# Room for GpSimd's DMA descriptors: 2048 in place of 16384 bytes of a partition

## The chip, the core and the metric

The kernel runs on one core of one Trainium2 chip. The metric is device microseconds of one execution. Before the change the median of three timed runs is 4273.25 us (4268.43 to 4274.99).

The engines are called PE (TensorE; PEld is its loading of weights), DVE (VectorE), ACT (ScalarE), POOL (GpSimd) and SP (SyncE). Each runs its own list of instructions in order, and they wait for one another by semaphores. SP, ACT and POOL also issue DMAs; all of those run on the core's 16 DMA engines.

## What is computed

Two layers on graphs: 8 graphs of 2048 nodes with 256 features, and an adjacency matrix of 0 and 1 per graph.

```python
h = maximum(layernorm(x), 0)
idx = first 25 neighbours of each node, by number
agg = max over them of h[idx]               # maximum(agg, 0) where a node has 25 or fewer
x = x + relu(concat(h, agg) @ W0 + b0)

h = maximum(layernorm(x), 0)
hidden = h @ W1.T
s = leaky_relu(hidden @ a1 [row] + hidden @ a2 [column])
x = x + softmax(s over neighbours) @ hidden + bias
```

## The kernel before

The 16384 nodes are handled in 32 quads of 512 rows, four tiles of 128 rows each (one row per partition). A step s of the main loop takes quad s through layer 0 and quad s - 4 through the attention of layer 1, so that from step 4 on both go on beside one another (`LAG`, `STEPS`, lines 34 and 59). Steps 0 to 3 have no attention; the attention of the last five quads is done in a part of its own behind the loop, where step 31's gathers are the last.

Layer 0 needs, for each node, the normalised features of its 25 neighbours. They lie in a table in HBM, and POOL fetches them (lines 470 to 525): for each of the four tiles of a quad it issues 25 indirect DMAs, called gathers here, one for each place k in the list of neighbours. A gather reads 128 rows of 1 KB, one into each partition, at the addresses in `idx[:, t, k]`. That makes 100 gathers in a step and 3200 in all. Tiles alternate between two buffers `near[:, 0]` and `near[:, 1]` and two semaphores `near_in[0]` and `near_in[1]`, and every gather adds 16 to its tile's semaphore when it has landed. The core of it:

```python
for k in range(S):
    attention(s, stages, t, k)
    pool.indirect_dma_start(
        out=near[:, t % 2, k, :], out_offset=None, in_=table,
        in_offset=bass.IndirectOffsetOnAxis(ap=idx[:, t, k:k + 1], axis=0),
    ).then_inc(near_in[t % 2], 16)
```

Ahead of a tile POOL waits until DVE has read the tile before the last out of the same buffer (`agg_made`), and ahead of tiles 0 and 2 for their indices (`idx_ready`). `attention(s, stages, t, k)` (line 476) adds further waits ahead of fixed gathers: POOL isn't to run ahead of certain marks of the attention. In steps 5 to 30 they stand in tile 0 ahead of k = 3, 8, 12 and 20 and in tile 1 ahead of k = 4, 9 and 21; in steps 4 to 30 in tile 2 ahead of k = 16 and 22 and in tile 3 ahead of k = 1, 8, 16 and 22. None stands ahead of k = 13, the 14th gather, or k = 14, the 15th, of any tile.

DVE takes the maximum over a tile's 25 neighbours as soon as all have landed (`maximum`, line 910: `near_in[t % 2]` has to reach 16 x 25 more than for the tile before in that buffer; its first instruction is line 914). PE multiplies by the weights (line 1266), DVE adds the residual (line 933). Meanwhile DVE searches the next quad's neighbours (lines 851, 857), ACT makes the masks from the adjacency (line 566), and attention runs in eight chunks: SP transposes masks by DMA (line 364), ACT and PE make the weights (lines 596, 602, 1325, 1326), PE the products (line 1333).

[...]

## Time and profile before

| | us |
|---|---|
| timed runs, median of three | 4273.25 |
| timed runs, lowest and highest | 4268.43, 4274.99 |
| profiled execution, its span (the only time that its page gives) | 5229.9 |
| busy in the profiled execution: POOL | 3056.0 |
| busy: PE, DVE, ACT | 2607.8, 2599.4, 1568.6 |
| idle time of POOL ahead of gathers | 1944.2 |

The span goes from the first to the last instruction of the profiled execution. That execution is 957 us longer than the median of the timed runs, so a share or a wait that it shows can't be taken over into a timed run as it stands. A gather's busy time on POOL is the making of its descriptors, not the transfer; when a tile has landed is seen from DVE, which waits for it.

### The profile page before, as it was taken

The page shows a single profiled execution, that of the slowest core. Times are in us where ns is not written, and L with a number is a line of the kernel's source. Part 1 is how long each engine was busy: PE and PEld are TensorE (multiplying, and loading weights), DVE is VectorE, ACT ScalarE, POOL GpSimd, SP SyncE. Part 2 cuts the span into 40 slices and gives each one's busy share as a digit, 9 for nine tenths or more (in the row PEclk, how much of TensorE's full clock was granted, in tenths as well). Part 3 has the DMA queues.
Part 4 walks back from the last instruction along what each step waited for, and adds up shares of the span by engine and source line. Part 5 has one row for each costly group of instructions (what it writes and reads, how often), then busy time and mean ns, then how long its engine had stood idle before and what let it go on. Part 6 is the DMA issues. An engine that isn't in the chain of part 4 may idle for free.

```text
span 5229.9 us, 38170 instructions
## 1 busy us (share of the span) xinstructions
PE 2607.8 (50%) x8674; PEld 1604.8 (31%) x8782; DVE 2599.4 (50%) x6725; ACT 1568.6 (30%) x1745; POOL 3056.0 (58%) x3204
## 2 busy tenths in 40 slices
PE   2122235556455455545555545555554555553479
PEld 0011113333233333333333323333332333332256
DVE  5444354454455454555445546545455554544432
ACT  3011123323333323333323333332333333232135
POOL 5565556666666566666656666666666665666510
PEclk6555557777666777667777766777766777776689
DMA  7344446556655555565655655665566565555320
GB/s 253 114 162 141 144 139 188 160 181 181 176 180 177 168 178 170 178 189 170 187 155 178 184 178 168 188 178 172 170 178 188 170 187 157 171 175 154 121 88 29
DMA packets 477228, 866.03 MB, mean 166 GB/s; under 512 B 308298, under 2 KB 309204, under 8 KB 456660
## 3 DMA queue, kind: packets, MB, share of 16 engines
q0 software_dynamic: 153600, 419.64, 28.2%
q1 hardware_dynamic: 305140, 378.64, 22.5%
q10 hardware_dynamic: 18432, 67.12, 3.3%
q8 instruction: 22, 0.36, 0.0%
q14 instruction: 34, 0.28, 0.0%
HBM read 690.98 MB, written 119.54 MB: 155 GB/s over the span
## 4 chain that ended last, share of the span: by engine, by line
PE 26%; issue 23%; another core or an unknown queue 22%; DVE 17%; ACT 8%; SPq 2%; DMA 1%; POOL 1%; ACTq 0%; DVEq 0%; POOLq 0%
PE acc L1333 13%; DVE highest L917 6%; DVE lin L941 3%; PE bank L1266 3%; ACT nm_t L566 2%; ACT wgt L602 2%; PE pen L1326 2%; DVE top L851 2%; PE pen L1325 1%; PE bank L1246 1%; DVE key L857 1%; ACT pen L596 1%; PE bank L1283 1%; SPq L364 1%
## 5 line engine op out<-in xcount | busy, mean ns | idle before, releaser
L521 POOL DMA_INDIRECT near<-table_dram,idx x3200 | 3055.8, 955 | 1944.2 <-issue 1000.3
L1333 PE MATMUL acc<-hid,wgt 128*128 (+1 forms) x4096 | 1187.2, 442 | 458.8 <-ACT wgt L602 380.9
L1333 PEld LDWEIGHTS acc<-hid,wgt 128*128 128x128 f32 x4096 | 889.6, 223 | 643.7 <-issue 435.2
L917 DVE TENSOR_TENSOR highest<-near,highest 128x512 f32<-128x512 f32 x1280 | 889.8, 695 | 167.5 <-DVE highest L917 75.9
L933 DVE SCALAR_TENSOR_TENSOR x_q<-bank,x_q 128x256 f32<-128x256 f32 x128 | 54.2, 423 | 1269.6 <-PE bank L1268 1052.9
L602 ACT ACTIVATE wgt<-pen,a_slope 128x512 f32<-128x512 f32 x448 | 305.5, 682 | 984.6 <-remote 522.7
L1266 PE MATMUL bank<-w_sb,h_t 128*128 128x256 f32 x1024 | 381.0, 536 | 422.8 <-ACT h_t L692 314.1
L566 ACT ACTIVATE nm_t<-adj_i,big_c 128x2048 bf16<-128x2048 int32 x128 | 501.1, 3942 | 7.3 <-DMA adj_i<-in_adj_dram 4.8
L941 DVE CUSTOM_DVE_ANT_0 lin<-acc,nm_q 128x2048 bf16<-128x2048 f32 x108 | 247.5, 2291 | 385.6 <-ACT acc L713 382.8
L1275 PE MATMUL acc<-cst,wgt 128*128 128x128 f32 x248 | 61.0, 427 | 750.6 <-ACT wgt L577 680.8
L1266 PEld LDWEIGHTS bank<-w_sb,h_t 128*128 128x128 f32 x1024 | 261.1, 268 | 508.5 <-ACT h_t L692 333.4
L851 DVE MAX8 top<-key 128x8 f32<-128x256 f32 (+1 forms) x1024 | 356.0, 388 | 114.2 <-remote 84.6
L596 ACT ACTIVATE pen<-a_b,a_rise 128x512 f32<-128x512 f32 x448 | 307.6, 691 | 198.4 <-DMA nm_c<-nm_q 98.0
L692 ACT ACTIVATE h_t<-bank 128x512 f32<-128x512 f32 x128 | 75.9, 593 | 909.3 <-PE bank L1260 454.1
L577 ACT ACTIVATE wgt<-x_q,shift,rstd 128x256 f32<-128x256 f32 x124 | 64.3, 590 | 761.7 <-DVE shift L801 418.7
L1325 PE MATMUL pen<-m_r,ones_b 3*128 3x512 bf16 x432 | 196.7, 455 | 182.1 <-issue 125.7
L857 DVE MATCH_REPLACE8 key<-top,key 128x256 f32<-128x256 f32 (+1 forms) x768 | 287.0, 382 | 0.0
L1275 PEld LDWEIGHTS acc<-cst,wgt 128*128 128x128 f32 x248 | 48.6, 223 | 756.7 <-ACT wgt L577 686.2
L1258 PE MATMUL bank<-cst,h_q 128*128 128x128 f32 x256 | 66.2, 350 | 376.7 <-DVE key L872 157.2
L1246 PE MATMUL bank<-nm_t,bit_w 128*128 128x512 bf16 x512 | 180.5, 512 | 107.7 <-ACT nm_t L566 50.8
L914 DVE TENSOR_TENSOR highest<-near 128x512 f32<-128x512 f32 x128 | 89.9, 703 | 175.4 <-DMA near<-table_dram,idx 131.4
L1300 PE MATMUL bank<-lin,ones_f 128*128 128x512 f32 x54 | 55.9, 1139 | 237.8 <-DVE x_q L933 229.3
(148 smaller groups left out, 2253.8 us busy)
## 6 DMA issues: line engine op xcount, KB each, us to landing
adj_i<-in_adj_dram SPq DMA_DIRECT2D x128, 1024.0 KB
nmask_dram<-nm_t ACTq DMA_DIRECT2D x128, 512.0 KB
nm_q<-nmask_dram SPq DMA_DIRECT2D x29, 2048.0 KB
near<-table_dram,idx POOLq DMA_INDIRECT x3200
h_q<-table_dram SPq DMA_DIRECT2D x32, 512.0 KB
x_q<-in_x_dram SPq DMA_DIRECT2D x32, 512.0 KB
xmid_dram<-x_q SPq DMA_DIRECT2D x32, 512.0 KB
o_q<-xmid_dram SPq DMA_DIRECT2D x32, 512.0 KB
```

The source lines that it names most:

```text
L521: pool.indirect_dma_start(out=near[:, t % 2, k, :], out_offset=None, in_=table, in_offset=bass.IndirectOffsetOnAxis(ap=idx[:, t, k:k + 1], ...
L566: nc.scalar.activation(nm_t[:, u, :].rearrange("p (q t r) -> p q t r", q=QB, t=T), by_tile, ACT.Relu, bias=BIG_B, scale=-BIG).then_inc(nm_ ...
L596: nc.scalar.activation(pen[:, j % 2, :], row, ACT.Relu, bias=rises[:, j:j + 1], scale=RISE).then_inc(lin_made, 1)
L602: nc.scalar.activation(wgt_part(j), pen[:, j % 2, :], ACT.Exp, bias=slopes[:, j:j + 1]).then_inc(wgt_made, 1)
L851: nc.vector.max(top[:, u, 8 * r:8 * r + 8], src[:, u, :]).then_inc(ix_step, 1)
L857: nc.vector.match_replace(src[:, u, :], top[:, u, 8 * r:8 * r + 8], src[:, u, :], PADKEY).then_inc(ix_step, 1)
L917: nc.vector.tensor_tensor(highest[:, :], pair(k), highest[:, :], ALU.max).then_inc(mx_step, 1)
L941: nc.vector.tensor_tensor_reduce(out=scratch, in0=scores, in1=non_edges[:, t, :], scale=1.0, scalar=-3.0e38, op0=ALU.subtract, op1=ALU.max ...
L1246: mm = nc.tensor.matmul(words, bit_w[:, k, :], members[:, :, k % T, :, k // T], start=(k == 0), stop=(k == GB - 1))
L1266: nc.tensor.matmul(bank1[:, 0:C], cat_t[:, k * P:(k + 1) * P], w0_sb[:, k, :], start=(k == 0), stop=False)
L1325: nc.tensor.matmul(pen[:, i, :], ones_b[:, :], m_r[:, :], start=False, stop=False, skip_group_check=True)
L1333: mm = nc.tensor.matmul(acc[:, t, 0:C + 1], wgt_part(j)[:, t * P:(t + 1) * P], hid[:, bass.ds(batch * NJ + j, 1), 0:C + 1].rearrange("p a ...
```

## The change

The program is made with an eighth of the room for descriptors of POOL's DMAs. [...] The instructions of all engines, their order and their waits stay as they are.

```diff
-    nc = _bacc.Bacc("TRN2", target_bir_lowering=False, num_devices=1)
+    nc = _bacc.Bacc("TRN2", target_bir_lowering=False, num_devices=1, dynamic_dma_scratch_size=2048)
```

## Rows read from the trace of the kernel before

**Rows 1.** The page: the span, and each engine's busy time, share and instructions.
```profile
span 5229.9 us, 38170 instructions
...
PE 2607.8 (50%) x8674; PEld 1604.8 (31%) x8782; DVE 2599.4 (50%) x6725; ACT 1568.6 (30%) x1745; POOL 3056.0 (58%) x3204
```

**Rows 2.** The page's costliest groups, the gathers: busy us, mean ns | idle before, main releaser.
```profile
L521 POOL DMA_INDIRECT near<-table_dram,idx x3200 | 3055.8, 955 | 1944.2 <-issue 1000.3
```

**Rows 3.** Timeline of POOL, two gathers: start, duration (us), instruction [idle before <-releaser].
```profile
2508.60 0.95 POOL L521 DMA_INDIRECT near<-table_dram,idx  x1 [0.31 <-issue]
2509.86 0.94 POOL L521 DMA_INDIRECT near<-table_dram,idx  x1 [0.30 <-issue]
```

**Rows 4.** Waits of POOL, longest first: us in total, times, longest.
```profile
POOL near L521 <- issue: 1000.3, 2990, 20.1
POOL near L521 <- remote: 290.2, 83, 5.0
POOL near L521 <- DVE agg L922: 222.6, 29, 26.1
POOL near L521 <- ACT hid L591: 128.9, 26, 8.0
```

**Rows 5.** All gathers of line 521: duration min/median/max (ns), first and last start (us).
```profile
L521 POOL DMA_INDIRECT near<-table_dram,idx x3200: 943/949/2351, 38.3 to 4999.5; - x189
```

**Rows 6.** Busy time in the last 230 us: PE, PEld, DVE, ACT, POOL, granted clock, DMA.
```profile
5000.00:5230.00 230.00, 204.32 (x1046) 140.21 (x1046) 72.41 (x190) 112.41 (x169) 0.44 (x1) 0.97 0.14 52
```

**Rows 7.** Timeline of POOL, 13th to 15th gather of steps 5 and 16.
```profile
832.73 0.95 POOL L521 DMA_INDIRECT near<-table_dram,idx  x1 [3.12 <-remote]
835.64 1.06 POOL L521 DMA_INDIRECT near<-table_dram,idx  x1 [1.97 <-issue]
837.01 0.95 POOL L521 DMA_INDIRECT near<-table_dram,idx  x1 [0.31 <-issue]
...
2531.37 0.95 POOL L521 DMA_INDIRECT near<-table_dram,idx  x1 [2.91 <-remote]
2534.28 1.22 POOL L521 DMA_INDIRECT near<-table_dram,idx  x1 [1.97 <-issue]
2535.80 0.95 POOL L521 DMA_INDIRECT near<-table_dram,idx  x1 [0.30 <-issue]
```

**Rows 8.** Timeline of POOL, 13th to 15th gather of step 4 (numbers 412 to 414).
```profile
663.78 0.94 POOL L521 DMA_INDIRECT near<-table_dram,idx  x1 [0.30 <-issue]
665.03 0.95 POOL L521 DMA_INDIRECT near<-table_dram,idx  x1 [0.30 <-issue]
666.29 0.95 POOL L521 DMA_INDIRECT near<-table_dram,idx  x1 [0.30 <-issue]
```

**Rows 9.** Timeline, the 25th gather of three tiles and DVE's start on each tile.
```profile
68.74 0.95 POOL L521 DMA_INDIRECT near<-table_dram,idx  x1 [0.30 <-issue]
...
71.61 0.70 DVE L914 TENSOR_TENSOR highest<-near 128x512 f32<-128x512 f32 x1 [10.30 <-DMA near<-table_dram,idx]
...
771.80 0.95 POOL L521 DMA_INDIRECT near<-table_dram,idx  x1 [0.30 <-issue]
...
775.94 0.70 DVE L914 TENSOR_TENSOR highest<-near 128x512 f32<-128x512 f32 x1 [4.96 <-DMA near<-table_dram,idx]
...
2471.34 0.95 POOL L521 DMA_INDIRECT near<-table_dram,idx  x1 [0.30 <-issue]
...
2474.54 0.70 DVE L914 TENSOR_TENSOR highest<-near 128x512 f32<-128x512 f32 x1 [5.29 <-DMA near<-table_dram,idx]
```

**Rows 10.** Timeline, a wait of POOL for ACT: the work waited for, and the gather.
```profile
2429.40 1.03 ACT L591 ACTIVATE hid<-acc 128x1032 f32 x1 [10.93 <-remote]
...
2431.20 0.95 POOL L521 DMA_INDIRECT near<-table_dram,idx  x1 [5.03 <-ACT hid L591]
```

**Rows 11.** Timeline of POOL, three further waits, in tiles 2, 3 and 1.
```profile
2461.31 0.95 POOL L521 DMA_INDIRECT near<-table_dram,idx  x1 [5.36 <-DVE agg L922]
...
2486.26 0.95 POOL L521 DMA_INDIRECT near<-table_dram,idx  x1 [3.94 <-remote]
...
2559.46 0.95 POOL L521 DMA_INDIRECT near<-table_dram,idx  x1 [5.17 <-DVE o_q L1010]
```

## The prediction

> **What bounds the kernel now.** I read the page's first part, then the waits of POOL, then the gathers one by one on the timeline. The span is 5229.9 us and no engine fills it: POOL, which generates the gathers' descriptors, is busy longest, 3056.0 us or 58% [rows 1]. Its line says more than its share: 3200 gathers of 955 ns, and 1944.2 us of idle time just before them, of which 1000.3 us is "issue", time in which it waited for nothing that the profile shows [rows 2]. On the timeline that idle time is 0.30 us between one gather and the next, so they come every 1.25 us (2509.86 - 2508.60) [rows 3]. The other 943.9 us are waits for DVE, ACT, PE and DMAs [rows 4].
>
> The profiled execution is 957 us longer than the 4273.25 us median of the timed runs, so some of what it shows is missing in a timed run. Two readings fit, and the forecast hangs on which is right.
>
> - **POOL paces the timed runs.** The first gather starts at 38.3 us, the last at 4999.5 us [rows 5]; behind it PE works alone, 204.32 us of 230 at a clock of 0.97 [rows 6]. With the gathers end to end, 38.3 + 3200 x 1.254 + 229.4 = 4280.5 us, 0.2% over the median (1.254 is the 1.25 of the timeline with one more digit: 0.949 busy, the median of the line, and 0.305 between). In this reading the 0.30 us belong to a gather, and the waits of POOL are what the profiler adds by slowing the others.
> - **POOL has slack.** If the 0.30 us were the profiler's, 3200 x 0.30 = 960 us would vanish and the 943.9 us of waits would stay: 5229.9 - 960 = 4270 us, which fits as well.
>
> I hold the first for likelier, about two to one: the gap is 0.30 or 0.31 us early and late alike, even where other engines' waits are long [rows 3, 7], which an inherent cost of the instruction would give, and the timed runs lie within 0.16% of each other.
>
> **What the change does.** No instruction is added, removed or moved on any engine; the room for descriptors is an eighth. How many gathers fit in the old room can be read off: in each of the steps 5 to 30 the 14th gather (number 513, 613, ... 3013 counted from 0, 26 times) starts 2.92 us after the 13th in place of 1.25 (835.64 - 832.73, 2534.28 - 2531.37), although the program has no wait between the two; the wait stands ahead of the 13th [rows 7]. In the steps 0 to 4, where no wait stands ahead of the 13th gather, the same place shows nothing: gather 413 starts at 665.03, 1.25 us after the one ahead [rows 8]. I read the extra 1.66 us as POOL taking back old room, visible where its queue of decoded gathers has just been emptied by a wait and hidden where it is ahead of itself. A pause that comes every 100 gathers, at place 13, fits a room that is full after 113 gathers and is then given back in one batch, up to the last gather of a tile (number 99): everything that the older tiles' semaphore counted. An eighth of 113 is 14.
>
> **The cost, step by step.** A tile is 25 gathers. With room for 14, the 15th gather of every tile finds the room full of 14 gathers of its own tile, all on one semaphore. If a batch is given back only when its last gather has landed, POOL must wait for the gather that it issued just before: one full stop per tile, 32 x 4 = 128 stops. (The second time that the room fills, at the 4th gather of the next tile, the batch ends with the old tile's 25th gather, three gathers or 3.8 us back, and the landing below is shorter; that stop I cost at nothing, covered by the gathers already in POOL's queue, and at up to 0.5 us each if it isn't.)
>
> The price of a full stop has no row of its own, so I take it from neighbours:
> - The landing: where DVE sits waiting for a tile, it starts 2.25 us after the 25th gather's generation ended (2474.54 - 2471.34 - 0.95). That is typical of the steps with attention; the least is 1.92 us (71.61 - 68.74 - 0.95), the most 3.19 us (775.94 - 771.80 - 0.95) [rows 9].
> - POOL's reaction: ACT ends the work that POOL waits for at 2430.43, the gather starts at 2431.20, 0.77 us later [rows 10].
> - Less the 0.30 us that would have passed anyway.
>
> So 2.25 + 0.77 - 0.30 = 2.72 us, times 128 = 348 us. Ends: 1.92 - 0.30 = 1.62 us if POOL reacts as fast as DVE (207 us), and 3.19 + 0.77 - 0.30 = 3.66 us (468 us). I take the middle, since most tiles of the run lie in steps like that of the 2.25. A gain isn't in this term: a stop can't make POOL faster. If POOL paces the run, all of it is exposed: 4273 + 348 = **4621 us**, between 4480 and 4741. Giving back 100 entries at once costs 1.66 us, so 14 cost some 0.23 us by proportion, 30 us over 128 stops, which lies inside the upper end. What is late next is the whole chain behind a tile (maximum, product, row's result), but all of it shifts with POOL and adds nothing.
>
> **The rivals.**
>
> *Covered.* With POOL in slack, each stop stands ahead of a wait that POOL makes anyway: 5.17, 5.03, 5.36 and 3.94 us at four places of one step [rows 10, 11]. A stop of 2.72 us disappears in each. Left are the tiles of the six steps without these waits or with few (0 to 4 and 31), 24 x 2.72 = 65 us, less 26 x 1.66 = 43 us for the pause that goes: 4295 us, up to 4450 where half of the stops meet no wait. For it: the waits are there; against it: the 4280.5 above.
>
> *Free as it drains.* The room may be reusable as soon as the DMA engines have taken a descriptor, or entry by entry from the oldest. The oldest of 14 was issued 14 x 1.25 = 17.5 us before and has long landed [rows 3, 9]. Then nothing waits: 4273 us, no change. So too if the number doesn't reach the chip. Against it: an entry-by-entry return would not pause once in 100 gathers [rows 7]. [...] No row here shows when a descriptor is taken, only when a tile has landed.
>
> *Faster.* If nothing waits for a landing, but the batches shrink from 100 entries to 11 and 14, the pause at the 14th gather goes. Its place is POOL's queue right behind the wait at the 13th [rows 7], its price 26 x 1.66 = 43 us, and it decides if the pause is in the timed runs too: 4273 - 43 = 4230 us.
>
> *Dearer bookkeeping.* If the 1.66 us are per return and not per entry, 128 full stops cost 212 us more, and the 128 short ones up to as much again: 4833 to 5045 us. Against it: the gather after a pause, and those of the early steps, show nothing of the kind [rows 7, 8].
>
> **How the numbers follow.** Full stops exposed 0.48 (4480 to 4741); covered 0.21 (4295 to 4450); no change 0.15; faster 0.06; dearer 0.10. The time is that of the first, 4621 us. The range runs from 4265, which takes in no change and covered, to 4745; left out are faster and dearer, 0.16. About 0.2%, or 8.5 us, is what a measurement of this kernel can tell from no change. Faster 0.06, the same 0.15, slower 0.48 + 0.21 + 0.10 = 0.79. The likeliest case's own range is 4480 to 4741.
>
> **What would show it.** In the profile after, the 15th gather of every tile should start 1.6 us or more later than 1.25 us behind the 14th, with no wait of the program there, 128 times; the pause at the 14th gather of a step should be gone; POOL's idle time ahead of gathers should grow, and its waits for others shrink by part of it, because the profiled execution has those waits to cover with. Its span may thus grow by less than the timed runs. Wrong would be: gathers at an even 1.25 us through the 15th (the room isn't held until landing), or the stops visible and the timed runs within 1% (POOL has slack).

## The result and the profile after

The change makes the kernel slower: 4792.47 us (median of four runs, 4783.77 to 4800.35) against 4274.12 us of the kernel before in the same comparison, a ratio of 1.1212 with a 95% interval of 1.1195 to 1.123. That is 518 us more. The forecast was 4621 us within 4265 to 4745: the direction and the mechanism hold, the size doesn't, and the time lies outside the range.

The profiled execution of the kernel after spans 4785.5 us, as long as its timed runs. That of before was 957 us too long, so its rows are no measure of where time went. One more execution of the unchanged kernel (below, *before again*) spans 4266.0 us, and stands here beside the change. First the page of after: span, busy time of the engines, shares of the chain that ended last, and the group of the gathers (busy, mean ns | idle before, releaser).

```profile
span 4785.5 us, 38170 instructions
...
PE 2519.7 (53%) x8674; PEld 1563.3 (33%) x8782; DVE 2584.8 (54%) x6725; ACT 1565.4 (33%) x1745; POOL 3050.3 (64%) x3204
...
POOL 54%; issue 31%; PE 7%; DVE 3%; DMA 3%; SPq 1%; ACT 1%; POOLq 0%; DVEq 0%; ACTq 0%
...
L521 POOL DMA_INDIRECT near<-table_dram,idx x3200 | 3050.1, 953 | 1538.4 <-issue 1495.7
```

The same lines of *before again*:

```profile
span 4266.0 us, 38278 instructions
...
PE 2452.2 (57%) x8782; PEld 1511.0 (35%) x8782; DVE 2591.1 (61%) x6725; ACT 1563.8 (37%) x1745; POOL 3060.4 (72%) x3204
...
POOL 33%; PE 23%; issue 14%; DMA 10%; DVE 10%; SPq 7%; ACT 2%; POOLq 0%; DVEq 0%; ACTq 0%
...
L521 POOL DMA_INDIRECT near<-table_dram,idx x3200 | 3060.2, 956 | 1012.4 <-issue 956.5
```

The reader is to see three things. POOL's busy time is the same (3060 and 3050 us, 956 and 953 ns of one gather): a gather keeps it busy no longer than before. All of the difference is idle time ahead of gathers, 1538.4 - 1012.4 = 526 us, for a span that grew by 519.5 us. And nearly all of it is "issue": POOL waits for nothing that the program asked for. (POOL and "issue" make 85% of the chain after and 47% in *before again*, where it passes through other engines too; that POOL sets the pace there is read from its even gaps and from the last two runs below, not from the chain.) The waits of POOL show how it is spread (us in total, times, longest), first of *before again*, then of after:

```profile
POOL near L521 <- issue: 956.5, 3140, 0.3
```

```profile
POOL near L521 <- issue: 1495.7, 3184, 6.5
```

Before, no such wait is longer than 0.3 us; that is the even gap of [rows 3], 3140 times. After, there are long ones, and the timeline shows where. This is step 17 of after, from the 14th gather of tile 2 to the 4th of tile 3 (start, duration in us, instruction [idle before <- releaser]; nine gathers of tile 2 are left out):

```profile
2531.24 0.96 POOL L521 DMA_INDIRECT near<-table_dram,idx  x1 [0.31 <-issue]
2534.66 1.33 POOL L521 DMA_INDIRECT near<-table_dram,idx  x1 [2.46 <-issue]
...
2543.97 0.90 SPq L356 DMA_DIRECT2D adj_i<-in_adj_dram  x2
...
2547.57 0.95 POOL L521 DMA_INDIRECT near<-table_dram,idx  x1 [0.30 <-issue]
2548.82 0.95 POOL L521 DMA_INDIRECT near<-table_dram,idx  x1 [0.31 <-issue]
2550.07 0.95 POOL L521 DMA_INDIRECT near<-table_dram,idx  x1 [0.30 <-issue]
2551.33 0.95 POOL L521 DMA_INDIRECT near<-table_dram,idx  x1 [0.30 <-issue]
2556.63 0.70 DVE L914 TENSOR_TENSOR highest<-near 128x512 f32<-128x512 f32 x1 [21.14 <-DMA near<-table_dram,idx]
2557.23 0.94 POOL L521 DMA_INDIRECT near<-table_dram,idx  x1 [4.95 <-issue]
```

There are up to two stops per tile. The *full stop* stands ahead of the 15th gather (2534.66), as forecast: 2.46 us in place of 0.30. The second, the *short stop*, stands ahead of the next tile's 4th gather (2557.23) and is here twice as long. Beside it stands what it waits for: DVE starts on the old tile at 2556.63, the moment its 25 gathers have landed, and POOL goes on 0.60 us later, at the event that the program makes only DVE wait for.

The packets of POOL's DMA queue, which the trace of after keeps as well (`q0 software_dynamic: 153600`), show the landing itself: 48 of each gather, 16 of them of 4 bytes each, taken here for its 16 semaphore increments. In the full stop above the last of them ends at 2533.63, 1.43 us behind the generation of the 14th gather, and POOL goes on at 2534.66, 1.03 us later. At all 128 full stops POOL goes on 0.96 to 2.44 us (median 1.00) after the last packet of the gather issued just before.

Taken over all 3200 starts, and counting by how much each distance exceeds 1.254 us: the full stops sum to 297.7 us (all 128 of them), the short ones to 230.8 us (85 of the 127 that could be are over 0.3 us), everything else to 9.3 us, 537.8 us in all. *Before again* has 22.2 us in all. So late starts of gathers account for 537.8 - 22.2 = 516 of the 518 us, and nearly all of them stand at these two places.

### The profile page after: what moved, and what is told of

Its sections match the earlier page's. It is cut to its first block, busy times and chain, and to the rows that moved or that the text cites. A ratio compares the mean times of both kernels' runs of the same rounds, so it can differ in the third digit from the quotient of the medians.

```text
span 4785.5 us, 38170 instructions
## 1 busy us (share of the span) xinstructions
PE 2519.7 (53%) x8674; PEld 1563.3 (33%) x8782; DVE 2584.8 (54%) x6725; ACT 1565.4 (33%) x1745; POOL 3050.3 (64%) x3204
## 3 DMA queue, kind: packets, MB, share of 16 engines
q0 software_dynamic: 153600, 419.64, 31.3%
## 4 chain that ended last, share of the span: by engine, by line
POOL 54%; issue 31%; PE 7%; DVE 3%; DMA 3%; SPq 1%; ACT 1%; POOLq 0%; DVEq 0%; ACTq 0%
POOL near L521 54%; PE acc L1333 4%; DVE highest L917 2%; DMA near<-table_dram,idx 1%; PE bank L1266 1%; DMA nm_c<-nm_q 1%; SPq L364 1%; PE pen L1317 0%; PE pen L1315 0%; PE bank L1246 0%; PE pen L1325 0%; PE pen L1326 0%; DMA nmask_dram<-nm_t 0%; ACT h_t L692 0%; PE bank L1258 0%
## 5 line engine op out<-in xcount | busy, mean ns | idle before, releaser
L521 POOL DMA_INDIRECT near<-table_dram,idx x3200 | 3050.1, 953 | 1538.4 <-issue 1495.7
L1333 PE MATMUL acc<-hid,wgt 128*128 (+1 forms) x4096 | 1047.1, 402 | 70.5 <-ACT wgt L602 57.6
L1333 PEld LDWEIGHTS acc<-hid,wgt 128*128 128x128 f32 x4096 | 813.6, 202 | 199.0 <-issue 70.4
L1266 PE MATMUL bank<-w_sb,h_t 128*128 128x256 f32 x1024 | 428.9, 591 | 108.6 <-ACT h_t L692 108.6
L1266 PEld LDWEIGHTS bank<-w_sb,h_t 128*128 128x128 f32 x1024 | 291.3, 298 | 211.3 <-ACT h_t L692 153.5
L1258 PEld LDWEIGHTS bank<-cst,h_q 128*128 128x128 f32 x256 | 35.8, 185 | 958.5 <-issue 555.3
```

The costliest lines, as they stand in the source:

```text
L521: pool.indirect_dma_start(out=near[:, t % 2, k, :], out_offset=None, in_=table, in_offset=bass.IndirectOffsetOnAxis(ap=idx[:, t, k:k + 1], ...
L1266: nc.tensor.matmul(bank1[:, 0:C], cat_t[:, k * P:(k + 1) * P], w0_sb[:, k, :], start=(k == 0), stop=False)
L1333: mm = nc.tensor.matmul(acc[:, t, 0:C + 1], wgt_part(j)[:, t * P:(t + 1) * P], hid[:, bass.ds(batch * NJ + j, 1), 0:C + 1].rearrange("p a ...
```

## The experiments

Theory A: a room of 2048 bytes holds 14 gathers, as worked out in the prediction from the pause of [rows 7]; a full room is given back in a batch up to the last gather that counts on the oldest semaphore in it; POOL waits until that gather has landed. Theory B: each return costs work, whatever it waits for. Theory C: the room's size or the place of the tensors makes gathers slower. The times of the kernel before were 4267.63 us (first four runs) and 4268.23 us (next four).

**More semaphores in the same small room.**

```diff
-        near_in = [sem("near_in0"), sem("near_in1")]
+        near_in = [[sem(f"near_in{u}_{c}") for c in range(5)] for u in range(2)]
-                        ).then_inc(near_in[t % 2], 16)
+                        ).then_inc(near_in[t % 2][k // 5], 16)
-                dve.wait_ge(near_in[t % 2], 16 * S * (2 * s + t // 2 + 1))
+                for c in range(5):
+                    dve.wait_ge(near_in[t % 2][c], 16 * 5 * (2 * s + t // 2 + 1))
```

> The room stays at 2048 bytes, but each tile's 25 gathers count on five semaphores, five gathers on each. Theory A (a full room is given back in one batch, up to the last gather that counts on the oldest semaphore in the room, and POOL waits for that gather's landing): POOL fills the room at the 15th gather as before, but the batch ends ten gathers or 12.5 us back, long landed; every stop goes, the first starts of gathers stand 1.25 us apart, time 4274 to 4290 us. Theory B (a return costs about 2.1 us of work whatever it waits for): five returns per tile, 640 in all, time 4274 + 640 x 2.1 = 5620 us. Theory C (the small room itself, or where the tensors lie behind it, makes the gathers slow): nothing changes, 4792 us.

Measured: 4275.74 us, 1.0014 of before (1.0005 to 1.0023). The 518 us are gone but for some 6 to 8 (by the ratio and by the medians). The same two places of step 17 in its timeline, the 14th and 15th gather of tile 2, and the 3rd and 4th of tile 3 with DVE's start (line numbers behind the edit are one higher):

```profile
2264.50 0.96 POOL L521 DMA_INDIRECT near<-table_dram,idx  x1 [0.30 <-issue]
2265.76 0.95 POOL L521 DMA_INDIRECT near<-table_dram,idx  x1 [0.30 <-issue]
...
2281.26 0.70 DVE L915 TENSOR_TENSOR highest<-near 128x512 f32<-128x512 f32 x1 [10.08 <-DMA near<-table_dram,idx]
2282.02 0.96 POOL L521 DMA_INDIRECT near<-table_dram,idx  x1 [0.30 <-issue]
2283.28 0.95 POOL L521 DMA_INDIRECT near<-table_dram,idx  x1 [0.30 <-issue]
```

Neither stop is left (10.6 us in all tiles together at the 15th gather, 3.1 at the 4th), in a program that differs from the change in the semaphores and DVE's waits for them alone and is made with the same 2048. That rules out B (more returns should cost more) and C at once: what costs is *which gather* POOL has to wait for.

**Other sizes.** Only the number in the constructor changes.

```diff
-    ... dynamic_dma_scratch_size=2048)
+    ... dynamic_dma_scratch_size=4096)
```

> Room for 28 gathers. Theory A: only the stop at the 4th gather of a tile is left (batch: the old tile's 25 gathers), none at the 15th. By the stops of the 2048 trace, 231 us in all at the 4th gather and 298 us at the 15th, the time is 4274 + 231 = 4505 us (4480 to 4540). Theory B: one return per tile, 128 x 2.1 = 269 us, 4543 us, with the stop in every tile, also in tile 2 of a step and in the steps 0 to 3, where the 2048 trace has none at the 4th gather. Theory C: evenly longer distances between gathers, no stop.

Measured: 4411.03 us, ratio 1.0338 (1.0322 to 1.0354), below A's range. The place is right and the size is not: the stops at the 4th gather sum to 144.6 us in place of 231, everything else to 15.4. In steps 5 to 30 the tiles 1, 2 and 3 show 1.39, 0.92 and 2.96 us on average and tile 0 0.03; with 2048 bytes it was tile 2 that showed nothing. Theory B, with a stop in every tile, fails. The same place of step 17:

```profile
2328.62 0.95 POOL L521 DMA_INDIRECT near<-table_dram,idx  x1 [0.30 <-issue]
2329.88 0.95 POOL L521 DMA_INDIRECT near<-table_dram,idx  x1 [0.30 <-issue]
...
2350.41 0.70 DVE L914 TENSOR_TENSOR highest<-near 128x512 f32<-128x512 f32 x1 [17.44 <-DMA near<-table_dram,idx]
2351.18 0.95 POOL L521 DMA_INDIRECT near<-table_dram,idx  x1 [3.93 <-issue]
```

The 15th gather (2329.88) follows without a stop, and the 4th of the next tile again starts right behind DVE.

> Room for 21 gathers. Theory A: one full stop per tile at the 22nd gather (batch: the 21 of its own tile, the last just issued), and a return at the 18th gather that waits for a gather 18 places back, so for nothing; no stop at the 4th or 15th. The gather at place 21 lands 1.6 to 3.7 us after its generation in the 2048 trace, 2.4 on average, so a stop costs 2.4 + 0.98 - 0.30 = 3.1 us in the steps with attention and 2.2 us in the six others: 104 x 3.1 + 24 x 2.2 = 375 us, time 4650 us (4560 to 4700), more than with 4096 bytes by the full stops. Theory B: two returns per tile, as with 2048: 4792 to 4812 us.

Measured: 4758.14 us, ratio 1.1137 (1.1117 to 1.1157), above A's range. Half as much room again as the change has, and nearly no gain. The place is right: 128 stops at the 22nd gather, 496.9 us, and 22.1 us elsewhere. The size is not: 3.9 us each in place of 2.9. In tile 1 of a step they take 6.93 us on average, in tile 3 2.24.

> Room for 56 gathers. Theory A: a return at the 7th gather of every second tile, whose batch ends with the 25th gather of the tile before, seven gathers or 8.8 us back; the latest landing there is some 6 us, so POOL waits for nothing: 4274 us within 0.2%, the distance at the 7th gather at most 0.5 us over 1.25. Theory B: 64 returns of 2.1 us: 4274 + 134 = 4408 us.

Measured: 4268.76 us, ratio 1.0005 (0.9996 to 1.0014), no pause at the 7th gather (0.8 us over the pace in all 128 tiles together). B, with 4408 us, falls a third time.

The run also sets theory A's wording right. The first stops of a tile with 1024, 2048 and 3072 bytes are at its 8th, 15th and 22nd gather, 7 gathers for each 1024 bytes, so 8192 bytes are taken, as an estimate, for 56. With these the room is first full with tiles 0 and 1 and six gathers of tile 2, and tile 2 counts on the semaphore of tile 0. By the letter of A ("the last gather that counts on the oldest semaphore in it") the batch would end with the 56th gather, just issued, and POOL would have to stop; gather 57 starts at 108.83 us, 1.25 us behind it and before its last packet ends at 110.02. The expectation's other wording, a batch up to the end of the tile before, fails in the run with five semaphores: read there as everything but the newest semaphore's gathers, a batch would end five gathers back, and at 71 of the 319 places POOL goes on less than 0.8 us after that gather's last packet, or before it, where no stop of these runs ends sooner than 0.87 us after the packet it waits for. What fits every run is the oldest *unbroken run* of gathers on one semaphore. Here that is a whole tile, whose last gather is 32 back, so this run doesn't show what a batch seven gathers back would cost.

> Room for 7 gathers. Theory A: three full stops per tile, at the 8th, 15th and 22nd gather, and the one at the 4th that waits for the old tile's 25th. With 2.2 us at the 8th and 15th, 3.9 at the 22nd (as in the run with 3072 bytes) and 1.8 at the 4th (as with 2048), 10.1 us per tile: 4274 + 128 x 10.1 = 5567 us (5350 to 5700). If the cost went with the number of gathers that fit, in a smooth way (twice the cost of 2048 for half the room): 4274 + 2 x 518 = 5310 us, with no stop of its own at the 8th and 22nd.

Measured: 5422.91 us, ratio 1.2704 (1.2683 to 1.2726), inside A's range. Four places show the stops: the 4th gather 62.1 us, the 8th 273.5, the 15th 387.2, the 22nd 444.6; the rest is 15.0, of which 11.9 are short delays (none over 1.1 us) at the 14th. Three stops of tile 2 of step 17 (8th, 15th, 22nd) and the two gathers that frame the missing one in the next tile (3rd and 4th):

```profile
2885.67 0.94 POOL L521 DMA_INDIRECT near<-table_dram,idx  x1 [2.34 <-issue]
...
2896.86 0.94 POOL L521 DMA_INDIRECT near<-table_dram,idx  x1 [2.33 <-issue]
...
2912.05 0.94 POOL L521 DMA_INDIRECT near<-table_dram,idx  x1 [6.75 <-issue]
...
2919.55 0.95 POOL L521 DMA_INDIRECT near<-table_dram,idx  x1 [0.30 <-issue]
2920.81 0.95 POOL L521 DMA_INDIRECT near<-table_dram,idx  x1 [0.30 <-issue]
```

The second of these full stops, one of the shortest, costs 2.0 us over the gap (2.33 - 0.30). The third is three times as long, and behind it the 25th gather lands in time, so the short stop drops out: here what makes landings late is paid once, by the stop that meets it.

**How far back the batch ends.**

```diff
-                        ).then_inc(near_in[t % 2], 16)
+                        ).then_inc(near_in[t % 2][min(k // 12, 1)], 16)
-                dve.wait_ge(near_in[t % 2], 16 * S * (2 * s + t // 2 + 1))
+                for c, n in enumerate((12, 13)):
+                    dve.wait_ge(near_in[t % 2][c], 16 * n * (2 * s + t // 2 + 1))
```

> Room 2048, two semaphores per tile: gathers 0 to 11 on one, 12 to 24 on the other. Theory A: at the 15th gather the batch ends with gather 11, three back, landed but in few places: that full stop (298 us) goes. At the 2nd gather of the next tile the room is full again, and its oldest semaphore ends with the old tile's 25th gather, now only two back: the stop moves from the 4th to the 2nd gather and grows by up to 2.5 us each, to some 4.5 us behind the ends of tiles 3, 0 and 2, and 1.4 us behind tile 1 and in the early steps. By landings of 5.3, 5.0, 1.9 and 5.7 us that is 17 us per step x 26 = 443, and 17 for the early steps: 4274 + 460 = 4735 us (4620 to 4790). Nothing at the 4th and 15th gathers. Theory C (the room's size alone): 4792, stops at the 4th and 15th.

Measured: 4731.29 us, ratio 1.1077 (1.1046 to 1.1109); 4735 were expected. The stops stand at the 2nd gather, 465.7 us (expected 460), the full stops are gone (15.4 us at the 15th gather, where the batch ends three gathers back). One of the stops at the 2nd gather, in tile 3 of step 17, 0.62 us behind DVE:

```profile
2507.07 0.70 DVE L915 TENSOR_TENSOR highest<-near 128x512 f32<-128x512 f32 x1 [20.14 <-DMA near<-table_dram,idx]
2507.69 0.94 POOL L521 DMA_INDIRECT near<-table_dram,idx  x1 [6.48 <-issue]
```

So doubling the semaphores brings little here, because it takes away the cheap wait (15.4 us left of 297.7) and leaves the dear one (465.7 us in place of 230.8), with less time in between; five take away both (10.6 and 3.1 us left).

**Why the old tile's 25th gather is late.** In after it starts at 2547.57, its generation ends 0.95 us later, and DVE sees the tile at 2556.63: 8.11 us. In *before again* the same gather ends at 2269.82 + 0.95, and DVE starts at 2273.04, 2.27 us later. The loads of the adjacency (line 356, twice 1 MB) are the suspects. In after they are issued at 2543.97, ahead of that gather; in *before again*, behind it:

```profile
2269.82 0.95 POOL L521 DMA_INDIRECT near<-table_dram,idx  x1 [0.30 <-issue]
...
2272.43 0.90 SPq L356 DMA_DIRECT2D adj_i<-in_adj_dram  x2
...
2273.04 0.70 DVE L914 TENSOR_TENSOR highest<-near 128x512 f32<-128x512 f32 x1 [10.30 <-DMA near<-table_dram,idx]
```

The windows of after (the stretch, its length, busy us of PE, PEld, DVE, ACT, POOL, then granted clock, share of the DMA engines, GB/s) around the full stop and the short one:

```profile
2530.00:2534.00 4.00, 4.00 (x11) 2.98 (x12) 3.96 (x16) 3.94 (x5) 1.89 (x2) 0.65 0.33 98
2548.00:2557.00 9.00, 5.66 (x21) 3.68 (x20) 0.37 (x1) 0.69 (x1) 3.37 (x4) 0.88 1.08 312
```

At the full stop a third of the DMA time is used, at the short one all of it. To try it, the loads were made smaller in the changed kernel; three quarters of each mask's columns are then not loaded and keep older values:

```diff
-                sp.dma_start(adj_i[:, t % 2, :], tile(adj_r, q, t)).then_inc(adj_in[t % 2], 16)
+                w = N if isinstance(q, int) else N // 4
+                sp.dma_start(adj_i[:, t % 2, 0:w], tile(adj_r, q, t)[:, 0:w]).then_inc(adj_in[t % 2], 16)
```

> Room 2048. The adjacency loads of the main loop (line 356) bring a quarter of their columns, 256 KB in place of 1 MB each, so most columns of a mask are those of an earlier tile; the neighbours found are others, and the count of instructions stays. Theory D: the stop at the 4th gather costs so much because the old tile's 25th gather lands among bulk loads; at the end of tile 2 those are the adjacency's. Its landing falls from 5.7 us to about 2, the stop at the 4th gather of tile 3 (3.10 us over the pace, on average of steps 5 to 30) falls under 0.8, 26 x 2.5 = 65 us, while tiles 0 and 1 (behind the ends of tiles 3 and 0, where other loads run) keep 2.9 and 2.4: 4792 - 65 = 4727 us (4700 to 4750). Theory E: the landing is late because of POOL's own queue or the transposes of masks; nothing changes, 4792 us.

Measured: 4668.59 us, ratio 1.0943 (1.0924 to 1.0961), 124 us under the change and more of a gain than the 65 expected. The stop at the 4th gather of tile 3 fell from 3.10 to 0.74 us, tile 1's stayed (2.37 and 2.28), and the full stops stayed (289.2 us). Tile 0's, expected to stay at 2.89, fell to 1.66 us as well, so D named the mechanism and not its whole reach. The same stop as above:

```profile
2488.94 0.94 POOL L522 DMA_INDIRECT near<-table_dram,idx  x1 [0.30 <-issue]
...
2493.95 0.70 DVE L915 TENSOR_TENSOR highest<-near 128x512 f32<-128x512 f32 x1 [17.91 <-DMA near<-table_dram,idx]
2494.55 0.94 POOL L522 DMA_INDIRECT near<-table_dram,idx  x1 [0.91 <-issue]
```

From the end of the 25th gather's generation to DVE's start it is now 4.07 us in place of 8.11, and the stop falls from 4.95 to 0.91 us, by the same 4.04. Landing and stop move one for one. But 4.07 isn't the 2 us that D expected: the adjacency is part of the cause, and the rest, for which the transposes of masks in the same stretch (theory E) stay a candidate, is open. In these two places the loads of SP make POOL's landing late (8.11 us beside the large ones, 4.07 beside the small) and don't block it; how the DMA engines share their time between the two was not shown. Which loads delay the ends of tiles 0 and 3, where other transfers run, was not tried.

**Does POOL pace the kernel before?** Two runs go to the reading on which the forecast was built.

```diff
             def attention(s, stages, t, k):
+                return
```

> Room 16384, as before the change, but POOL's waits for marks of the attention (the helper attention, line 476) are left out; its waits for buffers, indices and table rows stay. Theory P (POOL's pace of 1.25 us per gather fills the timed runs, and the waits that the profile of before shows in these places are in that profiled execution alone): 4270 us, within 0.4% of before, and the gathers 1.25 us apart throughout. Theory S (POOL has slack and the waits are in the timed runs): faster by a large part of their 780 us, 3600 to 4000 us, or slower by more than 1% if transfers collide that the waits kept apart.

Measured: 4269.16 us, ratio 1.0003 (0.9993 to 1.0012). Without the attention's marks, behind which most waits of [rows 4] stand, nothing changes, and its waits of POOL show the gap alone (the line number is one higher):

```profile
POOL near L522 <- issue: 974.2, 3198, 0.3
```

> The kernel before, unchanged, for one more profiled execution. If the 949.6 us by which its gathers fell behind an even 1.254 us belonged to that one profiled execution, this one spans 4260 to 4280 us, POOL's line shows waits of 0.3 us and no pause at the 14th gather of a step. If they belong to the kernel with the large room whenever it is profiled, it spans some 5230 us again, with the waits for DVE and ACT and the pause.

Measured: a span of 4266.0 us, and the waits shown at the top. The distances exceed 1.254 us by 22.2 us in all, and the pause at the 14th gather of a step [rows 7] is not there. The long waits and the pause belonged to that one profiled execution.

## Why the prediction was right in kind and wrong in size

- *POOL paces the timed runs, the 0.30 us belong to a gather, the waits are the profiler's.* Right, but for the last words: a second profiled execution of the same kernel lacks the waits, so profiling alone doesn't make them, and why the first one had them stays open. Every later execution with 8192 bytes or more shows the 0.3 us (the longest wait for "issue" of *before again*, *no_marks* and *room_8192*) and none of the waits, and leaving the program's marks out moves nothing (1.0003). That the sum of this reading, 4280.5 us, came within 0.2% of the timed median is in part luck: its 229.4 us of tail come from the long execution (193.8 us in *before again*), and it has none of the 22.2 us by which the gathers of *before again* fall behind the pace. Nor does PE work alone in that tail; ACT is busy for 112.41 of its 230 us and DVE for 72.41 [rows 6].
- *Room for 113 gathers, 14 after.* Right for 14: the stops stand at the 15th gather with 2048 bytes, the 22nd with 3072, the 4th of the next tile with 4096, the 8th with 1024. That is 7 gathers for each 1024 bytes, and by it, as an estimate, 16384 bytes hold 112. The count of 113 was never seen to cost anything, but it led to the 14. The batch of 100 gathers that went with it, up to gather 99, isn't shown: by the rule that fits the runs a batch would be one tile, 25 gathers.
- *A batch goes back up to the last gather of a semaphore, and must have landed.* Right in the small rooms, and the part best shown: semaphores alone move the stops (two per tile) or remove them (five). It has to be read as the oldest unbroken run on one semaphore, as the room of 8192 bytes shows.
- *Full stop, 128 x 2.72 = 348 us.* Right in kind, 17% high: 297.7 us, 2.33 each. The stop of step 17 shown above is 2.46 - 0.30 = 2.16 us. With the 0.60 us by which POOL follows DVE, that is a landing of 2.46 - 0.60 = 1.86 us by DVE's measure, where 2.25 were taken from a tile's 25th gather (0.39 us of the difference), and a reaction of 0.60 where 0.77 were taken (0.17 us); the DMA engines are a third busy there (0.33 from 2530 to 2534 us).
- *The second refill, "covered by the gathers already in POOL's queue, and at up to 0.5 us each if it isn't".* **This is the step that failed.** It measured 230.8 us, 1.80 per tile. The batch does end with the old tile's 25th gather, but three gathers' head start (3.8 us) isn't more than its landing, which took 8.11 us beside the adjacency loads. The landing times used, 1.92 to 3.19 us, came from an execution whose waits had moved gathers and loads against each other [rows 9]: by the packets, tile 1's 25th gather lands 1.5 us after its generation in the profiled execution of before, on average of steps 5 to 30, 5.0 us in *before again* and 2.1 after, tile 2's 1.9, 2.1 and 5.5. And the cover did not show: no gather starts during a stop (none from 2551.33 to 2557.23). The queue of decoded gathers, by which the prediction also explained the place of the pause, was the author's reading; no run shows it.
- *Tail shifts and adds nothing.* Right: from the last gather's start to the end it is 197.5 us after and 193.8 in *before again* (4785.5 - 4588.0 and 4266.0 - 4072.2).
- The rivals: *covered* fell with the waits that were to cover; *free as it drains* is not what the chip does here, since at all 128 full stops POOL stands still until 0.96 us or more after the landing. When a descriptor is taken is not shown; the 14th gathers of after, whose packets stand apart from others' in 127 of 128 tiles, have their first packet 0.69 us or more behind the end of their busy time on POOL; *faster* fell, for the pause is not in timed runs; *dearer bookkeeping* came nearer in time (4833 to 5045 us) for the wrong reason: with 8192 bytes returns show no cost (0.8 us in all at the 7th gathers), and with five semaphores the many more of them cost 2 to 10 us in all (the interval of the ratio).
- Among the signs to look for, "its span may thus grow by less than the timed runs" failed with the disturbed profile that it rested on.

With the measured terms put in, the sum is 4274 + 298 + 231 + 9 - 22 = 4790 us; measured 4792.

## What to carry to other kernels

Count in gathers how much the room for POOL's descriptors holds (here 7 for each 1024 bytes), and ask of the batch that is given back when it fills which gather ends it and how long ago that was issued: at ten gathers back (five semaphores) or 32 (8192 bytes) a return showed next to no stop (10.6 and 0.8 us in all), at three back (two semaphores) it cost 15.4 us in all, and at one, two and four back it cost what was left of the landing (297.7, 465.7 and 230.8 us in all). In a small room, spread the gathers over several semaphores (a few gathers on each) before asking for more room: here five per tile bought back all but 6 to 8 of 518 us with the same 2048 bytes. And take a landing time from the stretch in which the wait will stand, with its bulk loads, from an execution as long as the timed runs.

## What was not expected of the hardware

- The cost does not fall smoothly with the room: 1024, 2048, 3072, 4096 and 8192 bytes give 5423, 4792, 4758, 4411 and 4269 us. At 3072 bytes the one full stop stands ahead of the 22nd gather, and at 3.9 us each it costs nearly as much as both stops of 2048 bytes (4.1 us together).
- A POOL held by its full room goes on soon after DVE starts on the same landing (0.60 us from 2556.63 to 2557.23, 0.77 us from 2350.41 to 2351.18), although no wait on that semaphore stands in POOL's program there. At the 4th gather this time is nearly always the same within a run and grows with the batch: 0.52 us with 1024 bytes (4 gathers go back), 0.60 with 2048 (11), 0.76 or 0.77 with 4096 (25). By these three, as an estimate, a return that POOL stands waiting for takes some 12 ns for each gather in it.
- One profiled execution was 957 us longer than the timed runs and put most of the difference down to waits that no other execution shows.
